# Moving the experts' weight splits beside the first attention layer, a later gate, and gathers four tiles ahead

## What is computed

```python
xn = _layernorm(x)
x = x + _L0_gnn_ref(xn, edge_index, ...) + _L0_mix_ref(xn[None], ...)[0]     # relu attention, 16 heads
x = x + _L0_ffn_ref(_layernorm(x)[None], w_gate, w_up, w_down)[0]
xn = _layernorm(x)
x = x + _L1_gnn_ref(xn, edge_index, edge_type, ...) + _L1_mix_ref(xn[None], ...)[0]   # linear attention
x = x + _L1_ffn_ref(_layernorm(x)[None], Wg, W1, b1, W2, b2)[0]

def _L1_ffn_ref(input, Wg, W1, b1, W2, b2):            # 8 experts, the best 2 of each node
    probs = softmax(input @ Wg)
    top_vals, top_idx = top_k(probs, 2)                # scores: top_vals / sum(top_vals)
    h = relu(einsum('ebsd,edh->ebsh', xm, W1) + b1)    # 1024 -> 256
    y = einsum('ebsh,ehd->ebsd', h, W2) + b2           # 256 -> 1024
    return sum(y * scores)
```

## Time and profile before

| | us |
|---|---|
| median of 3 runs | 2580.04 |
| lowest, highest | 2578.36, 2588.32 |
| profiled execution | 2584.9 |
| its span | 2583.1 |
| PE busy | 2284.2 (88%) |
| DVE busy | 1377.8 (53%) |
| POOL busy | 1232.5 (48%) |
| ACT busy | 734.2 (28%) |

### The profile page before, as it was taken

How to read it: one execution, slowest core, us unless ns; L and a number is a source line. 1 busy time by engine, 2 the same in 40 slices (tenths; PEclk the granted TensorE clock), 3 DMA queues, 4 the chain that set the end, 5 groups by cost and what they waited for, 6 DMA issues and landing times.

```text
span 2583.1 us, 40475 instructions
## 1 busy us (share of the span) xinstructions
PE 2284.2 (88%) x15976; PEld 1538.7 (60%) x15976; DVE 1377.8 (53%) x2374; ACT 734.2 (28%) x1252; POOL 1232.5 (48%) x834
## 2 busy tenths in 40 slices
PE   6999999999998799897888979989999998956887
PEld 5565464464457666663344557756777777844554
DVE  5845536525669699983333451344576564344332
ACT  4244435525652222231013141321111211131222
POOL 6576454373027412103540395038888876312554
PEclk8999999999999899997889999989999999967999
DMA  3312202211203300022000102214434421355775
GB/s 126 87 35 48 47 18 48 48 23 42 79 9 111 113 18 17 17 83 102 17 17 1 43 21 64 75 59 128 120 92 143 122 77 42 144 208 172 133 129 101
DMA packets 99531, 192.20 MB, mean 74 GB/s; under 512 B 22457, under 2 KB 62528, under 8 KB 92966
## 3 DMA queue, kind: packets, MB, share of 16 engines
q1 hardware_dynamic: 82518, 161.00, 19.6%
q0 software_dynamic: 16848, 28.91, 6.7%
HBM read 120.83 MB, written 53.50 MB: 67 GB/s over the span
## 4 chain that ended last, share of the span: by engine, by line
PE 65%; DVE 14%; issue 7%; POOL 6%; DMA 4%; ACT 3%; DVEq 0%; SPq 0%; POOLq 0%; ACTq 0%
PE ps L480 14%; PE ps L482 14%; PE ps L483 14%; DMA WR<-rows_split,SR 3%; PE pt L680 3%; PE ps L832 2%; DVE SR L745 2%; PE pt L832 2%; PE pt L681 2%; PE ps L664 2%; PE ps L663 2%; DVE SR L1671 2%; ACT SR L710 1%; DVE SR L1783 1%; POOL WR L1358 1%
## 5 line engine op out<-in xcount | busy, mean ns | idle before, releaser
L480 PE MATMUL ps<-WR,RB 128*128 128x256 f16 (+2 forms) x2120 | 610.3, 288 | 39.7 <-DVE SR L1671 19.0
L482 PE MATMUL ps<-WR,RB 128*128 128x256 f16 (+2 forms) x2120 | 609.4, 287 | 0.0
L483 PE MATMUL ps<-WR,RB 128*128 128x256 f16 (+2 forms) x2120 | 608.5, 287 | 0.0
L1351 POOL TENSOR_TENSOR WR<-WR,units 128x2048 f32<-128x2048 f32 (+2 forms) x36 | 148.3, 4119 | 430.8 <-PE ps L480 408.1
L745 DVE SCALAR_TENSOR_TENSOR SR<-ps,SR 128x512 f16<-128x512 f32 (+1 forms) x480 | 274.5, 589 | 86.4 <-ACT SR L710 69.7
L710 ACT ACTIVATE SR<-ps 128x512 f16<-128x512 f32 (+1 forms) x480 | 246.0, 519 | 113.3 <-PE ps L664 94.2
L480 PEld LDWEIGHTS ps<-WR,RB 128*128 128x128 f16 x2120 | 212.7, 100 | 90.1 <-issue 16.4
L480 PE MATMUL ps<-RB,WR 128*128 128x512 f16 (+1 forms) x720 | 247.1, 343 | 10.6 <-DVE RB L432 7.4
L482 PE MATMUL ps<-RB,WR 128*128 128x512 f16 (+1 forms) x720 | 246.9, 343 | 0.0
L483 PE MATMUL ps<-RB,WR 128*128 128x512 f16 (+1 forms) x720 | 246.6, 342 | 0.0
L483 PEld LDWEIGHTS ps<-WR,RB 128*128 128x128 f16 x2120 | 212.8, 100 | 46.6 <-issue 1.7
(11 more groups left out here) (330 smaller groups left out, 4284.8 us busy)
## 6 DMA issues: line engine op xcount, KB each, us to landing
SR<-in_w_moe SPq DMA_DIRECT2D x64, 256.0 KB, 3.6
moe_split<-RB SPq DMA_DIRECT2D x128, 128.0 KB, 1.8
RB<-moe_split SPq DMA_DIRECT2D x8, 2048.0 KB, 12.9
RB<-RB SPq DMA_DIRECT2D x96, 156.2 KB
WR<-in_w_mix SPq DMA_DIRECT2D x12, 1024.0 KB
WR<-in_w_mix SPq DMA_DIRECT2D x8, 1536.0 KB
RB<-in_x SPq DMA_DIRECT2D x18, 512.0 KB, 5.9
WR<-in_w_out SPq DMA_DIRECT2D x8, 1024.0 KB
```

The costliest lines, as they stand in the source:

```text
L480: m = nc.tensor.matmul(o, ah, bh, start=(k == 0), stop=False)
L482: nc.tensor.matmul(o, ah, bl, start=False, stop=False)
L483: m = nc.tensor.matmul(o, al, bh, start=False, stop=(k == n - 1))
```

## The change

- **Gate.** At step i of the loop PE computes the gate of tile i-5, no longer of i-4, and writes the logits into the spare columns of the ring bank that the next `out1` tile will use (after `wait_ring`). DVE copies the logits of tiles 0 to 3 one by one inside its loop, before the evacuation of the same bank, and those of tiles 4 to 9 from one bank (`GB`) at the end.
- **Gathers.** Five buffers for three; four gathers are issued at the start, and for tile t the gather of t+4. The gather of t waits for the transposes of t-5.
- **Block number.** PE reads the block number of t+2 between the two halves of `down(t)`, where it read that of t+1 just before `up(t+1)`.
- **Routing.** Four DVE instructions for the block numbers (L2150 to L2153) stand behind the index list, where they stood before it.
- **Pieces.** The 64 pieces are split during mix0. POOL does `pieces_of(p)` (9 pieces each for p = 1 to 6, 10 for p = 7) after split 3, 5, 6, 8, 9, 11 and 12 and the edge DMAs behind it; SP loads and saves them after `shuffle(p)`. The buffers are the unused last third of `wst`, `wh` and `wl`. In mix1 POOL and SP do only the slots.

```diff
-        xg = [WR(4096 * j, F16, 2, DIM) for j in range(3)]
+        xg = [WR(4096 * j, F16, 2, DIM) for j in range(3)] + [SR(S1 + 4096 * j, F16, 2, DIM) for j in range(2)]
+        NG = len(xg)
...
+        def pieces_of(p):
+            return range((p - 1) * PIECES // (PAIRS - 1), p * PIECES // (PAIRS - 1))
...
                 out1(3, i)
                 if i >= 3:
                     turn3(i - 3)
-                if i == 4:
+                if i == 5:
                     pe.wait_ge(gate_split, 1)
-                if i >= 4:
-                    gate(i - 4)
+                if i >= 5:
+                    t = T0 + 3 * NT + i + 1
+                    wait_ring(pe, t)
+                    gate(i - 5, t % 4)
             for i in range(NT - 3, NT):
                 turn3(i)
-                gate(i - 1)
-            gate(NT - 1)
+                gate(i - 2, GB)
+            for i in (NT - 2, NT - 1):
+                gate(i, GB)
...
                     g.indirect_dma_start(edges_d, bass.IndirectOffsetOnAxis(pos[:, t:t + 1], 0),
                                          rec[:, t, :], None).then_inc(e_moved, 16)
+                for p in range(1, PAIRS):
+                    if n == (3 * p + 4) // 2:
+                        for k in pieces_of(p):
+                            piece(k)
             split(12, 0, 2048)
+            for k in pieces_of(PAIRS - 1):
+                piece(k)
...
-            for j in range(PAIRS):
-                split(28 + j, j % 2, 3072)
-                for p in range(j * PIECES // PAIRS, (j + 1) * PIECES // PAIRS):
-                    piece(p)
+            split_loop(28, 8, 3072)
...
             def gather(t):
-                if t >= 3:
-                    pool.wait_ge(xt_done, t - 2)
+                if t >= NG:
+                    pool.wait_ge(xt_done, t - NG + 1)
...
-            for t in range(3):
+            for t in range(NG - 1):
                 gather(t)
...
-                if t + 3 < MT:
-                    gather(t + 3)
+                if t + NG - 1 < MT:
+                    gather(t + NG - 1)
...
                 shuffle(sp, p, p % 2)
+                if p == 1:
+                    for k in range(2):
+                        piece_load(k)
+                for k in pieces_of(p):
+                    piece_save(k)
+                    if k + 2 < PIECES:
+                        piece_load(k + 2)
...
             for k in range(NT):
+                if k >= 6:
+                    t = TILE0["mix1_out"] + 3 * NT + k
+                    dve.wait_ge(mm_done, t + 1)
+                    logits(slice(k - 6, k - 5), t % 4)
                 out1(3, k)
```

More of the change, by code:

```diff
@@ L210, in build_program @@
         er = [SR(2048 * j, F32, 512) for j in range(4)]
-        pst = [SR(S1 + 25640, F32, PIECE), SR(8192, F32, PIECE)]
-        psh = [R0(SCR + 5160 + 2048 * s, F16, PIECE) for s in range(2)]
-        psl = [R0(SCR + 6184 + 2048 * s, F16, PIECE) for s in range(2)]
+        pst = [wst[:, 2048 + PIECE * s:2048 + PIECE * (s + 1)] for s in range(2)]
+        psh, psl = [w[:, 2048:2048 + PIECE] for w in wh], [w[:, 2048:2048 + PIECE] for w in wl]
         XM = [[SR(S1 + 4096 * j + 2048 * h, F16, KD, TN) for h in range(2)] for j in range(3)]
@@ L360, in build_program @@
         blk_loaded = [sem(f"blk_loaded{e}") for e in range(NE)]
-        xg_loaded = [sem(f"xg_loaded{j}") for j in range(3)]
+        xg_loaded = [sem(f"xg_loaded{j}") for j in range(NG)]
         xt_done, xt_hi, xt_lo = sem("xt_done"), sem("xt_hi"), sem("xt_lo")
@@ L1007, in _, with gate @@
                     out1(c, i)
-            def gate(i):
+            def gate(i, b):
                 pe.wait_ge(turn_lo, r3 + i + 1)
-                _, m = three(ps[0:TN, 0, 256 + i * NE:256 + (i + 1) * NE],
+                _, m = three(ps[0:TN, b, 256 + i * NE:256 + (i + 1) * NE],
                              [(XM[i % 3][0][:, k], XM[i % 3][1][:, k], wg_h[:, k], wg_l[:, k]) for k in range(KD)])
@@ L1395, in _, with piece @@
                     split_low(0, 2048)
+            def piece(p):
+                s = p % 2
+                pool.wait_ge(pw_loaded[s], 16 * (p // 2) + 16)
+                ch.link(g.tensor_tensor(pst[s], pst[s], units[:, 2:3].to_broadcast([128, PIECE]), ALU.mult))
+                if p >= 2:
+                    pool.wait_ge(pw_saved[s], 32 * (p // 2))
+                ch.link(g.tensor_tensor(psh[s], pst[s], units[:, 3:4].to_broadcast([128, PIECE]), ALU.mult))
+                g.tensor_tensor(psl[s], pst[s], psh[s], ALU.subtract).then_inc(pw_split, 1)
             split(1, 1, 2048)
@@ L1555, in _ @@
                 shuffle(sp, p, p % 2)
+                if p == 1:
[5 more added lines that the diff above has]
+                        piece_load(k + 2)
+            for s in range(2):
+                sp.wait_ge(pw_saved[s], 16 * PIECES)
             sp.wait_ge(shuffled, SHUF * PAIRS)
@@ L1604, in _ @@
                                  ).then_inc(c_loaded[r], 16)
[L1606 to L1626, removed]
-                        piece_load(p + 2)
-            for s in range(2):
-                sp.wait_ge(pw_saved[s], 16 * PIECES)
+            with sp.Fori(0, PAIRS) as i:
+                load(sp, i + SLOT0["mix1_qkv"], wst, one(A["w_mix1"][bass.ds(i, 1)]))
+            load(sp, SLOT0["mix1_out"], wst[:, 0:2048], A["w_out1"][0])
             sp.wait_ge(evac, TILE0["mix1_out"])
@@ L2070, in _ @@
             ch.link(v.memset(sel, 0.0))
-            ch.link(v.tensor_scalar(gs[0], ps[0:TN, 0, 256:256 + NT * NE].rearrange("p (i e) -> p i e", e=NE),
-                                    1.0 / (XS * WS), None, ALU.mult))
+            ch.link(logits(slice(4, NT), GB))
             ch.link(v.tensor_reduce(g1[0], gs[0], AX.X, ALU.max))
@@ L2149, in _ @@
             m.then_inc(hotf_ready, 1)
+            ch.link(v.tensor_scalar(spare_q, iota_tf, upto[:, NE - 1:NE], row_q, ALU.is_ge, ALU.mult))
+            dve.wait_ge(route_done, 1)
+            ch.link(v.tensor_tensor(id_f, ps[:, 2, 0:MC], spare_q, ALU.add))
+            v.tensor_copy(idx, id_f).then_inc(idx_ready, 1)
             ch.link(v.tensor_tensor(tile_e, along(iota_tf, NE), each(first_t, MC), ALU.is_ge))
@@ L2153, in _ @@
             ch.link(v.tensor_reduce(exp_f, tile_e, AX.X, ALU.add))
-            ch.link(v.tensor_scalar(spare_q, iota_tf, upto[:, NE - 1:NE], row_q, ALU.is_ge, ALU.mult))
-            dve.wait_ge(route_done, 1)
-            ch.link(v.tensor_tensor(id_f, ps[:, 2, 0:MC], spare_q, ALU.add))
-            v.tensor_copy(idx, id_f).then_inc(idx_ready, 1)
             v.tensor_copy(blk_i, blk_f)
```

35 lines of the change are left out of this document (19 added, 16 removed).

## The result

| | before | changed |
|---|---|---|
| median, us | 2579.93 (4 runs) | 2564.24 (4 runs) |
| lowest, highest | 2578.36, 2588.32 | 2560.74, 2567.42 |
| profiled execution's span | 2583.1 | 2562.9 |

What follows compares the result with a forecast made beforehand. It took PE (88% busy) as the bound, with waits in the gate loop, experts' loop and mix1. Gate -31, gathers -24, routing -1, mix1 -12 and pieces in mix0 +52 gave -16 on 2580.0: about 2564 us, range 2545 to 2590.

Runs made afterwards that it cites:

- loads_ahead: The changed kernel with SP issuing the next slot's load ahead of the batch of pieces, not behind it: 2520.93 us, 0.9773 of the kernel before.

## What to carry over

Where work is moved beside a stage with idle time, idle time on average doesn't say that it fits: write for each queue what is needed next and how long until then, and put the work behind the step with the longest time left. A load that feeds the critical engine goes ahead of the filler's DMAs on its queue; here that order alone was worth 38 us. And let a helper engine finish below the main engine's period: over it, its long instructions slide to where they hurt.

## What was new about the hardware

- POOL instructions over 128x512 beside DVE's two-operand additions cost PE nothing measurable (12 of them for each slot: 371.4 against 371.3 us), though they held DVE for 7 us in all (105.7 us of additions for 98.4). The three of 128x3072 for each slot did cost PE time once they lay beside short tiles. DVE's additions then took 148.9 us for 98.4; 36 us of that are long holds (107.0 for 70.6 us in additions of over 2 us), the rest short ones beside the pieces.
- After a stop of 27 us, PE ran at a granted clock of 0.50 for about 5.5 us; such a stop thus costs some 3 us more than it shows where nothing behind it absorbs them. After stops of 15.7 and 14.9 us it was 10 and 12 matmuls of 0.43 us, and 10 in `loads_ahead` after one of 5.7 us; after one of 0.3 us there were none.
- Two kernels with the same mix0 show the same 20 us of attention at a clock of 0.91 and of 1.00, PE being as busy: a term below 5 us can't be read from one pair of profiles.
